# Attention scores on Trainium2: fp32 score products of two heads at once, or of one head each into the two halves of the PSUM rows

## The chip, the cores and the metric

The kernel runs on one core of one Trainium2 chip. The metric is the device time in microseconds, the median of several runs. A core has five engines that run side by side and meet at semaphores: TensorE (PE in the profile, with its weight loads in a row of their own, PEld), VectorE (DVE), ScalarE (ACT), GpSimd (POOL) and SyncE (SP), which here only issues DMAs.

## The reference

A gated cross-attention block with 32 sequences of 64 tokens, model width 512, followed by a gated expert layer. Cut to what matters here:

```python
q = (layernorm(x) @ wq)   # 32 heads of 128
k = (ctx @ wk)            # 8 heads of 128, each shared by 4 query heads
v = (ctx @ wv)
q, k = rope(q), rope(k)
raw = einsum('bhqd,bhkd->bhqk', q, k) / sqrt(128)     # 64 x 64 for each sequence and head
attn = softmax(raw + mask, axis=-1)
x = x + tanh(g_xattn) * (einsum('bhqk,bhkd->bhqd', attn, v) @ wo)
x = x + tanh(g_ffn) * experts(layernorm(x))           # top-1 of 8, rank 16
```

All of it is fp32. Most products are split by hand into a high and a low part (three products of type fp32r for each fp32 one); the score products are not: they take q and k as plain fp32.

## The kernel before, in words

A first stage (up to about 205 us of the profile) makes keys and values for all sequences, stores them to DRAM, and normalises and turns x. Then comes a loop of 64 steps (`STEPS`). A step k stands for one KV head (a group of four query heads), and four sequences (`SUB_SEQS`); two steps share the same eight sequences (`chunk`), and four steps the same half of the batch and the same KV head. 16 groups by 4 steps are the 64.

Each engine has its own program, written out by hand, and all waits are on named semaphores. On TensorE (from line 801) a step is, in this order: `scores(k)` (line 881), `times_values(k-1)` (line 909: probabilities of the step before by the values), one or two products of the next group's q projection (`product`, line 849), `project_out(k-1, 0)` (line 935: the first 128 tokens of the step before by wo), more of the q projection, `turn_probs(k)` (line 898: four transposes), `project_out(k-1, 1)`, and the last products of the projection (lines 1046 to 1072). The last four steps have an order of their own (lines 1074 to 1131), without projections. The expert layer's routing products (line 983) and its other pieces are put between these parts in some steps.

`scores(k)` waits for q and k of its group (semaphores `rope_added`, `k_in`) and until VectorE has taken the scores before (`masked`). The bank `score` has 128 partitions by 512 columns: partitions 0 to 63 hold the first head of a pair, partitions 64 to 127 the second, and the columns are two head pairs (`hp`) by four sequences (`b`) by 64 keys. For each of the 8 (hp, b), one call multiplies the queries of two heads (stationary, 128 rows of the head width by 2 x 64 columns) by the 64 keys of the sequence (moving). The last call increments `scored`.

VectorE waits for `scored` in `mask_scores` (line 1231; line 1241 scales and adds the mask, line 1246 finds the maximum), GpSimd subtracts it (line 1870), ScalarE takes the exponential (line 1613), VectorE sums and inverts (lines 1250, 1252), GpSimd multiplies (line 1875), and TensorE transposes the probabilities in `turn_probs`. The rope of q ends in line 1180 on VectorE.

`TWIN_ROWS` (line 44) is `(slice(0, SEQ), slice(SEQ, 2 * SEQ))`, the two halves of the partitions.

Of the kernel before, what the change touches and what calls it, by code (L numbers as in the profile page):

```python
# [14 lines left out]
BATCH, SEQ, DM = 32, 64, 512  # L15
# [28 lines left out]
TWIN_ROWS = (slice(0, SEQ), slice(SEQ, 2 * SEQ))  # L44
# [116 lines left out]
def products_of(k):  # L161

    G, r = divmod(k, 4)
    if G + 1 == GROUPS:
        return [[], [], []]
    b = HEAD_PAIRS * (G + 1) + r // 2
    lots = ((0, 1), (2,), (3,)) if r % 2 == 0 else ((4, 5), (), (6,) if k + 1 < WIDE else ())
    return [[(b, i) for i in lot] for lot in lots]
# [32 lines left out]
Q_SLOT, Q_BEFORE = {}, {}  # L201
# [91 lines left out]
def build(nc, x, ctx, mask, g_attn, g_ffn, wq, wk, wv, wo, routed_w, lora_b, table, out):  # L293
# [8 lines left out]
    with ExitStack() as stack:  # L302
        def bank(name):
            return stack.enter_context(nc.psum_tensor(name, [P, 512], F32))
# [4 lines left out]
        def sb_at(offset, name, shape, dt=F32):  # L309
            return nc.alloc_sbuf_tensor_at(name, shape, dt, offset=offset)  # L310
# [13 lines left out]
        k_r = sb_at(base + 28672, "k_r", [P, 2, CHUNK])  # L324
# [9 lines left out]
        q_r = [sb_at(base + place, f"q_r{i}", [P, CHUNK_SEQS, 2, SEQ])  # L334
               for i, place in enumerate((98304, 102400, 106496, 110592, 94208, 118784))]
# [52 lines left out]
        small, score, turned = bank("small"), bank("score"), bank("turned")  # L388
# [151 lines left out]
        def chunk_of(u):  # L540
            G, c = divmod(u, CHUNKS)
            return G, c, (G // KV_HEADS) * CHUNKS + c
# [258 lines left out]
        def _(e):  # L801
            drained = {}

            def free(b):

                if b.name in drained:
                    e.wait_ge(*drained[b.name])
# [73 lines left out]
            def scores(k):  # L881
                u, s = divmod(k, SUBS)
                G, c, index = chunk_of(u)
                e.wait_ge(rope_added, ROPE_NO["q", HEAD_PAIRS * G + 1, 1 if c == 0 else 3] + 1)
                e.wait_ge(k_in[u % 2], 16 * (u // 2 + 1))
                if k:
                    e.wait_ge(masked, k)
                free(score)
                for hp in range(HEAD_PAIRS):
                    for b in range(SUB_SEQS):  # L890
                        seq = s * SUB_SEQS + b
                        col = (hp * SUB_SEQS + b) * SEQ
                        two_heads = q_r[Q_SLOT[G, hp, c]][:, seq, :, :].rearrange("p h s -> p (h s)")
                        last = e.matmul(score[:, col:col + SEQ], two_heads, k_r[:, u % 2, seq * SEQ:(seq + 1) * SEQ],  # L894
                                        start=True, stop=True)
                last.then_inc(scored, 1)

            def turn_probs(k):
# [126 lines left out]
            for n in range(len(JOBS)):  # L1025
                make(n)
                if n == X_TURN:
                    e.wait_ge(table_in, 16)
                if n - X_TURN in X_BESIDE:
                    turn_x(X_BESIDE[n - X_TURN])  # L1030
                for b, i in Q_AFTER.get(n, ()):
                    product(b, i)
                if n == SCORES_AFTER:
                    drained[score.name] = rope_added, ROPE_NO[JOBS[-4]] + 1
                    scores(0)
# [3 lines left out]
            first, middle, last = products_of(0)  # L1039
            for b, i in first + middle:  # L1040
                product(b, i)
            turn_probs(0)
            scores(1)
            for b, i in last:
                product(b, i)
            for k in range(1, WIDE):
                first, middle, last = products_of(k)
                if k > 1:
                    scores(k)
                between(k, 0)  # L1050
                times_values(k - 1)
                between(k, 1)
                for b, i in first[:1]:
                    product(b, i)
                between(k, 2)
                for b, i in first[1:]:
                    product(b, i)
                between(k, 3)
                project_out(k - 1, 0)
                between(k, 4)  # L1060
                for b, i in middle:
                    product(b, i)
                turn_probs(k)
                between(k, 5)
                project_out(k - 1, 1)
                between(k, 6)
                for b, i in last[:1]:
                    product(b, i)
                between(k, 7)
                for b, i in last[1:]:  # L1070
                    product(b, i)
                between(k, 8)
# [959 lines left out]
```

## Time and profile before

| | us |
|---|---|
| median of 3 runs | 1091.02 |
| lowest, highest | 1090.81, 1091.05 |
| span of the profiled execution, first to last instruction | 1089.0 |
| busy in it: PE, PEld | 1082.4, 919.3 |
| busy: DVE, ACT, POOL | 874.1, 636.8, 591.9 |

The profile has one execution. The time of that execution outside its span isn't known by itself; the median of the runs is 2.0 us above the span. PE's busy time is that of matmuls as recorded: they are pipelined, one starts before the record of the one before has ended, and their ends are modelled, so the distance between starts tells more than a record's length. PEld (weight loads) goes on beside PE. A plain fp32 matmul call leaves two records on each of the two rows; a call of type fp32r leaves one. A chain of waits is followed back from the last instruction, at each step to what released it.

### The profile page before, as it was taken

How to read it: one execution, taken by the hardware profiler on the slowest of the kernel's cores; microseconds unless marked ns; L12 is line 12 of the kernel's file. 1: busy time of each engine (PE TensorE's matmuls, PEld its weight loads, DVE VectorE, ACT ScalarE, POOL GpSimd, SP SyncE). 2: the span in 40 equal slices, each digit the busy share in tenths (PEclk: the TensorE clock that was granted, in tenths of full speed). 3: DMA queues.
4: the chain of work that ended last, by engine and by line, in shares of the span. 5: the costliest groups of instructions: out<-in, count | busy, mean ns of one | idle time of the engine just before them, and what ended most of it. 6: DMA issues, size and time to landing. Idle time of an engine off the chain costs nothing.

```text
span 1089.0 us, 17107 instructions
## 1 busy us (share of the span) xinstructions
PE 1082.4 (99%) x5640; PEld 919.3 (84%) x5640; DVE 874.1 (80%) x1423; ACT 636.8 (58%) x1112; POOL 591.9 (54%) x518
## 2 busy tenths in 40 slices
PE   9999999999999999999999999999999999999998
PEld 7888888888888888888888888888888888888886
DVE  7876657888888888888887898777777777777887
ACT  7563476586666666666655545555555555555553
POOL 5552379888877777777754433333333333333423
PEclk9999999999999999999999999999999999999999
DMA  7858964496646464646489546553535353543112
GB/s 258 273 210 336 391 220 183 155 379 201 214 155 213 155 213 156 212 156 212 141 300 380 185 136 205 177 187 111 187 110 187 112 184 114 179 116 118 40 39 78
DMA packets 106087, 206.27 MB, mean 189 GB/s; under 512 B 8849, under 2 KB 58641, under 8 KB 100113
## 3 DMA queue, kind: packets, MB, share of 16 engines
q1 hardware_dynamic: 105424, 204.40, 55.2%
q8 instruction: 47, 0.77, 0.3%
q10 hardware_dynamic: 576, 0.79, 0.2%
q14 instruction: 40, 0.32, 0.1%
HBM read 122.31 MB, written 82.84 MB: 188 GB/s over the span
## 4 chain that ended last, share of the span: by engine, by line
PE 97%; DVE 2%; DMA 0%; issue 0%; ACT 0%; DVEq 0%; SPq 0%
PE attn L945 32%; PE proj L877 28%; PE score L894 10%; PE attn L839 8%; PE score L839 4%; PE turned L839 4%; PE attn L930 3%; PE attn L932 3%; PE turned L905 3%; PE proj L811 1%; PE small L983 1%; PE small L1008 1%; PE score L983 0%; DMA near_raw<-in_ctx 0%; DVE o_s L1270 0%; DVE stats L1140 0%
## 5 line engine op out<-in xcount | busy, mean ns | idle before, releaser
L945 PE MATMUL attn<-wo_s,o_s 128*128 128x512 f32 x1524 | 374.7, 395 | 0.2 <-DVE o_s L1270 0.2
L877 PE MATMUL proj<-xB,wq_s 128*128 128x512 f32 x1344 | 332.6, 391 | 0.0
L945 PEld LDWEIGHTS attn<-wo_s,o_s 128*128 128x128 f32 x1524 | 280.9, 188 | 57.0 <-DVE o_s L1270 0.4
L877 PEld LDWEIGHTS proj<-xB,wq_s 128*128 128x128 f32 x1344 | 252.0, 188 | 51.3 <-issue 0.2
L1863 POOL TENSOR_TENSOR rot<-rot,tab 128x512 f32<-128x512 f32 x110 | 162.3, 1475 | 145.2 <-ACT rot L1584 145.0
L1633 ACT ACTIVATE o_s<-attn 128x512 fp32r<-128x512 f32 x127 | 69.3, 595 | 112.2 <-PE attn L932 112.1
L894 PEld LDWEIGHTS score<-k_r,q_r 128*128 128x128 f32 x1024 | 123.9, 191 | 5.5 <-DVE q_r L1180 0.4
L1175 DVE TENSOR_TENSOR q_r<-q_r,tab 128x512 f32<-128x512 f32 x127 | 120.9, 952 | 1.5 <-ACT x_third L1584 1.4
L894 PE MATMUL score<-k_r,q_r 128*128 128x64 f32 x1024 | 121.3, 271 | 0.0
L1605 ACT ACTIVATE copies<-proj 128x512 f32<-128x512 f32 x96 | 57.5, 599 | 78.0 <-PE proj L877 77.8
L1282 DVE SCALAR_TENSOR_TENSOR acc<-attn,gates_t,acc 128x512 f32<-128x512 f32 x127 | 94.8, 747 | 4.1 <-PE attn L945 1.2
L1863 POOL TENSOR_TENSOR rot_third<-rot_third,tab 128x512 f32<-128x512 f32 x40 | 61.3, 1533 | 57.6 <-ACT rot_third L1584 54.8
L1262 DVE TENSOR_TENSOR p_low<-turned,p_high 64x512 fp32r<-64x512 f32 x128 | 87.7, 686 | 5.2 <-ACT p_high L1621 2.8
L1621 ACT ACTIVATE p_high<-turned 64x512 fp32r<-64x512 f32 x128 | 75.6, 590 | 23.5 <-PE turned L905 21.8
L1583 ACT ACTIVATE rot<-q_r 64x512 f32<-64x512 f32 x84 | 52.4, 623 | 52.5 <-DVE q_r L1219 51.4
L1270 DVE TENSOR_TENSOR o_s<-attn,o_s 128x512 fp32r<-128x512 f32 x127 | 81.4, 680 | 1.8 <-ACT o_s L1633 1.7
L1624 ACT ACTIVATE p_high<-p_high 64x512 fp32r<-64x512 f32 x128 | 80.8, 631 | 2.8
L1219 DVE TENSOR_TENSOR q_r<-copies,proj 128x512 f32<-128x512 f32 x127 | 81.1, 678 | 0.3 <-issue 0.3
L1180 DVE TENSOR_TENSOR q_r<-q_r,rot 128x512 f32<-128x512 f32 x85 | 69.2, 814 | 6.0 <-POOL rot L1863 0.3
L1241 DVE SCALAR_TENSOR_TENSOR prob_odd<-score,mask_sb 128x512 f32<-128x512 f32 x32 | 22.1, 691 | 52.7 <-PE score L894 52.6
L1870 POOL TENSOR_TENSOR prob_odd<-prob_odd,neg_max 128x512 f32<-128x512 f32 x32 | 33.7, 1053 | 54.9 <-DVE neg_max L1246 54.0
L1870 POOL TENSOR_TENSOR prob_even<-prob_even,neg_max 128x512 f32<-128x512 f32 x32 | 33.5, 1047 | 48.5 <-DVE neg_max L1246 48.5
(269 smaller groups left out, 1681.5 us busy)
## 6 DMA issues: line engine op xcount, KB each, us to landing
wq_kept<-wq_s SPq DMA_DIRECT2D x16, 1792.0 KB, 6.3
wq_s<-wq_kept SPq DMA_DIRECT2D x16, 1792.0 KB, 8.2
v_kept<-vst SPq DMA_DIRECT2D x64, 256.0 KB, 4.3
v_s<-v_kept SPq DMA_DIRECT2D x128, 128.0 KB, 5.0
wo_kept<-wo_s SPq DMA_DIRECT2D x32, 512.0 KB, 5.7
wo_s<-wo_kept SPq DMA_DIRECT2D x32, 512.0 KB, 5.2
k_kept<-kst SPq DMA_DIRECT2D x32, 256.0 KB, 2.2
wq_raw<-in_wq SPq DMA_DIRECT2D x16, 512.0 KB, 7.8
```

What stands on the lines that cost most here:

```text
L839: last = e.matmul(b[:, :], stationary, moving, start=(kt == 0 and m == 0), stop=(kt == KT - 1 and m == 2))
L877: last = e.matmul(dst[:, :], wq_s[:, b % 2, A, s, kt, :], xB[:, B, mv, kt, :], start=(first and kt == 0 and m == 0), stop=(kt == 1 and m = ...
L894: last = e.matmul(score[:, col:col + SEQ], two_heads, k_r[:, u % 2, seq * SEQ:(seq + 1) * SEQ], start=True, stop=True)
L945: last = e.matmul(out_bank(k, bp)[:, :], o_s[:, s, bp, h, :], wo_s[n % WO_SLOTS][:, m, :], start=(h == 0 and i == 0), stop=(h == GROUP - 1 ...
L1175: e.tensor_tensor(dst, src, cos, ALU.mult).then_inc(times_cos, 1)
L1219: e.tensor_tensor(q_tile(b, j) if dst is None else dst, by_seq(copies[:, copy, :]), by_seq(proj[PRODUCTS[i][2]][:, :]), ALU.add).then_inc( ...
L1262: e.tensor_tensor(p_low[rows, :, twin, :], turned[rows, :].rearrange("p (b n) -> p b n", b=PAIRS), p_high[rows, twin, :].bitcast(F32).rear ...
L1270: e.tensor_tensor(low, src, high.bitcast(F32), ALU.subtract).then_inc(out_low, 1)
L1282: e.scalar_tensor_tensor(out=acc[:, tile, :], in0=out_bank(k, bp)[:, :], scalar=gates_t[:, 0:1], in1=acc[:, tile, :], op0=ALU.mult, op1=AL ...
L1621: e.activation(p_high[rows, twin, :], turned[rows, :], ACT.Copy).then_inc(probs_high, 1)
L1624: last = e.activation(p_high[TWIN_ROWS[1 - twin], twin, :], p_high[rows, twin, :].bitcast(F32), ACT.Copy)
L1863: e.tensor_tensor(r3, r3, sin, ALU.mult).then_inc(times_sin, 1)
```

## The change

In `scores`, the call for two heads becomes two calls for one head each. The stationary operand has 64 columns instead of 128, the moving operand (the keys) is the same, and the output is the first or the second half of the bank's partitions. The semaphore increment stays on the last call.

```diff
@@ -890,9 +890,10 @@
                     for b in range(SUB_SEQS):
                         seq = s * SUB_SEQS + b
                         col = (hp * SUB_SEQS + b) * SEQ
-                        two_heads = q_r[Q_SLOT[G, hp, c]][:, seq, :, :].rearrange("p h s -> p (h s)")
-                        last = e.matmul(score[:, col:col + SEQ], two_heads, k_r[:, u % 2, seq * SEQ:(seq + 1) * SEQ],
-                                        start=True, stop=True)
+                        keys = k_r[:, u % 2, seq * SEQ:(seq + 1) * SEQ]
+                        for head, rows in enumerate(TWIN_ROWS):
+                            last = e.matmul(score[rows, col:col + SEQ], q_r[Q_SLOT[G, hp, c]][:, seq, head, :], keys,
+                                            start=True, stop=True)
                 last.then_inc(scored, 1)
```

## Rows read from the trace of the kernel before

**Rows 1.** The page: busy time with share and instructions, and slices of the span.

```profile
span 1089.0 us, 17107 instructions
PE 1082.4 (99%) x5640; PEld 919.3 (84%) x5640; DVE 874.1 (80%) x1423; ACT 636.8 (58%) x1112; POOL 591.9 (54%) x518
...
PE   9999999999999999999999999999999999999998
...
PEclk9999999999999999999999999999999999999999
```

**Rows 2.** The page: the chain that ended last, by engine and by line.

```profile
PE 97%; DVE 2%; DMA 0%; issue 0%; ACT 0%; DVEq 0%; SPq 0%
PE attn L945 32%; PE proj L877 28%; PE score L894 10%; PE attn L839 8%; PE score L839 4%; PE turned L839 4%; PE attn L930 3%; PE attn L932 3%; PE turned L905 3%; PE proj L811 1%; PE small L983 1%; PE small L1008 1%; PE score L983 0%; DMA near_raw<-in_ctx 0%; DVE o_s L1270 0%; DVE stats L1140 0%
```

**Rows 3.** Groups by shape on PE and PEld: count | busy us, mean ns | idle before.

```profile
L945 PE MATMUL attn<-wo_s,o_s 128*128 128x512 f32 x1524 | 374.7, 395 | 0.2 <-DVE o_s L1270 0.2
L877 PE MATMUL proj<-xB,wq_s 128*128 128x512 f32 x1344 | 332.6, 391 | 0.0
L894 PE MATMUL score<-k_r,q_r 128*128 128x64 f32 x1024 | 121.3, 271 | 0.0
...
L894 PEld LDWEIGHTS score<-k_r,q_r 128*128 128x128 f32 x1024 | 123.9, 191 | 5.5 <-DVE q_r L1180 0.4 <-issue 0.3
...
L905 PEld LDWEIGHTS turned<-tab,prob_even 128*128 128x128 f32 x128 | 15.7, 139 | 4.4 <-POOL prob_even L1875 0.4
```

**Rows 4.** The chain in order of time, 505 to 530 us: start, us, what.

```profile
506.35 0.44 PE turned L905 x4
506.79 2.77 PE attn L945 x12
509.56 1.36 PE proj L877 x6
510.92 1.73 PE score L894 x16
512.65 0.29 PE attn L930 x2
...
523.66 1.73 PE score L894 x16
```

**Rows 5.** Timeline of PE and PEld around one step's scores: start, us.

```profile
506.54 3.02 PE L945 MATMUL attn<-wo_s,o_s 128*128 128x512 f32 x12
509.40 1.52 PE L877 MATMUL proj<-xB,wq_s 128*128 128x512 f32 x6
510.76 1.89 PE L894 MATMUL score<-k_r,q_r 128*128 128x64 f32 x16
512.46 0.49 PE L930 MATMUL attn<-p_high,v_s 128*128 128x256 f32 x2
...
506.51 2.62 PEld L945 LDWEIGHTS attn<-wo_s,o_s 128*128 128x128 f32 x12
...
510.53 1.98 PEld L894 LDWEIGHTS score<-k_r,q_r 128*128 128x128 f32 x16
...
518.72 0.58 PEld L905 LDWEIGHTS turned<-tab,prob_odd 128*128 128x128 f32 x4
...
510.53 0.41 PEld L894 LDWEIGHTS score<-k_r,q_r 128*128 128x128 f32 x2
```

**Rows 6.** Routing products, fp32 with 136 columns: timeline, and their group by shape.

```profile
1079.68 1.09 PE L983 MATMUL score<-routedT,last_s 128*128 128x136 f32 x8
...
L983 PE MATMUL score<-routedT,last_s 128*128 128x136 f32 x8 | 1.1, 279 | 0.0
```

**Rows 7.** Timeline, the first products after TensorE's rest at 6 us.

```profile
6.46 0.30 PEld L839 LDWEIGHTS score<-ctxT,wk_s 128*128 128x128 f32 x2 [1.43 <-DVE ctxT L1170]
...
6.49 1.17 PE L839 MATMUL score<-ctxT,wk_s 128*128 128x512 f32 x4 [1.02 <-DVE ctxT L1170]
```

**Rows 8.** Waits (us in total, times, longest), and timeline of DVE and POOL at one step.

```profile
DVE prob_odd L1241 <- PE score L894: 52.6, 25, 2.3
...
DVE prob_even L1241 <- PE score L894: 24.3, 25, 1.6
...
508.75 0.67 DVE L1180 TENSOR_TENSOR q_r<-q_r,rot_third 128x512 f32<-128x512 f32 x1
...
512.69 0.69 DVE L1241 SCALAR_TENSOR_TENSOR prob_odd<-score,mask_sb 128x512 f32<-128x512 f32 x1 [1.76 <-PE score L894]
...
516.93 1.05 POOL L1875 TENSOR_TENSOR prob_odd<-prob_odd,row_inv 128x512 f32<-128x512 f32 x1 [0.46 <-DVE row_inv L1252]
```

**Rows 9.** Windows by stage: length, busy PE, PEld, DVE, ACT, POOL, clock, DMA share, GB/s.

```profile
205.00:1040.00 835.00, 834.74 (x4465) 714.10 (x4464) 685.83 (x1080) 498.62 (x864) 458.77 (x384) 1.00 0.54 180
```

## The prediction, made before the changed kernel ran

> **What bounds the kernel now.** I began with the page's busy table and its slices [rows 1]: TensorE is busy for 1082.4 of 1089.0 us at the full granted clock in all 40 slices, VectorE for 80%. The chain that ended last [rows 2] runs over TensorE for 97% and over the score products (line 894) for 10%. Busy TensorE is not TensorE at its peak, so the next view is the costliest groups by shape [rows 3]: the two big groups wait 0.2 us in all, so what the score products give or take on TensorE moves the end by the same amount, as long as nobody else becomes late. The chain in order of time [rows 4] shows one step of the loop: it comes back every 12.74 us (510.92 to 523.66), and 1.73 us of it are the score products. They are 8 calls and stand as 16 records, since each fp32 product is recorded as two weight loads and two matmuls. 64 steps by 1.73 us are 110.7 us, the chain's 10%.
>
> **What bounds the score products themselves.** The timeline of the two PE rows [rows 5] has 16 loads in 1.98 us. The second starts 0.23 us after the first (the two together end at 510.94, less one's 0.19 us), the last at 512.51 - 0.19 = 512.32, so 14 gaps cover 1.56 us: 0.111 us from load to load. What would the matmul alone need? The routing products are fp32 as well, with 136 columns [rows 6]: 8 records in 1.09 us, (1.09 - 0.28) / 7 = 0.116 us each, 0.85 ns per column; 64 columns would need 0.055 us. Their loads, of the same 128x128 as the score's, fit into those 0.116 us. So here the weight load sets the pace and the matmul half of the array's time is empty: per record 0.111 us of load against 0.055 us of stream. Instruction issue is not seen to bind: after rest a load starts at 6.46 and its matmul at 6.49, 0.03 us apart [rows 7]. That is just the pace that the change could ask for at best, so it stays a weak point.
>
> **The change, part by part.** Each of 512 products becomes two with 64 stationary columns instead of 128 and the same 64 moving columns. Records go from 16 to 32 a step on each PE row, 1024 to 2048 in all. The keys stream twice. The same rows and columns of the score bank are written in the end, the one semaphore increment still comes with the last product, and no wait, DMA or instruction of another engine is added or moved.
>
> Loads: no row shows a 64-column load. Bounds: 0.111 us each if a load costs the same whatever its width, 0.055 us if it goes by columns. I take 0.055, since two loads of the trace that differ only in mode (a transpose's, 139 ns, and a product's, 191 ns) [rows 3] show that the duration follows the amount that is moved and not a fixed price. Matmuls: 0.055 us each, as above.
>
> Without any overlap between the halves a step is 32 x 0.056 = 1.79 us against 1.73: +0.06 us. With overlap, where the product for rows 0 to 63 and that for rows 64 to 127 use different columns of the array at the same time, two records share a slot. The order is upper, upper, lower, lower (two records per call), so in order starts still allow it: the second record of one half runs beside the first of the other. That is 32 x 0.028 = 0.90 us. No row shows two products side by side, so the bounds are 0.90 and 1.79; I take 0.90 because there is nothing in common that is full: load and stream of one half fill their slot, and those of the other half are on other columns. The Trainium skill's page "TensorE: Matmul & The Clock Gate", section "Part 3: Packing small matmuls", measured 2.38x for three column tiles; scaled to two that is about 1.6x, 1.13 us a step by an estimate, which would halve my gain. No run here shows it.
>
> Switching: 64 times the array goes from whole to half use and back. Nothing in the trace switches. Lower bound 0, if the next load is taken in beside the running matmul, as the first score load is now (it starts at 510.53, and the matmul before it runs on to 510.76). Upper bound: the array is emptied. A matmul record of 512 columns lasts 0.39 us while the next one starts 2.77 / 12 = 0.23 us after it [rows 3, 4], so 0.16 us are its tail, and after rest the first weights lie open: four matmuls took 1.17 us where 3 x 0.23 + 0.39 = 1.08 are usual [rows 7], 0.09 us. Together 0.25 us per switch, 0.50 us per step. The Trainium skill's page "TensorEngine Tiling (Array Packing)", section "Key Properties", says that a change of tiling mode drains TensorE; that speaks for the upper end, and the trace can't confirm it. I take 0.15 us a switch, 0.30 a step, since the tail and the load may partly lie over each other.
>
> Sum per step: 0.90 + 0.30 = 1.20 us against 1.73, so 0.53 us less; by 64 steps 34 us.
>
> **Does it arrive?** VectorE takes the scores. It stood waiting for them in 25 + 25 steps for 52.6 + 24.3 us [rows 8], 1.5 us each, and in the step shown for 1.76 us. Scores that come 0.53 us sooner are taken sooner. From there mask, maximum, exponential and normalisation run until 516.93 + 1.05 = 517.98 [rows 8], and the transposes of the probabilities begin on TensorE with the load at 518.72 [rows 5]; both the chain and TensorE's other work begin at the end of the scores, so this slack of 0.7 us stays as it is. VectorE is busy 685.8 of 835 us between 205 and 1040 us [rows 9]; with 34 us less it stands at 86%. The rope sums that the next scores need end at 508.75 + 0.67 = 509.42 [rows 8], 1.1 us ahead of the first score load. If the cover goes, in the 14 steps where VectorE doesn't wait, about 3 us of the 34 are lost. Forecast: 31 us less. The sum is made against the profiled execution (span 1089.0 us); the median of the runs is 1091.0, 2 us around the span that stay. 1091 - 31 = 1060 us.
>
> **Rivals.**
> *The halves take turns and the switches are paid.* Place: lines 894 ff., 64 times. Step 1.79 + 0.30 = 2.09 us, +0.36 a step, +23 us, 1114 us; with the dear switch +0.56, +36 us, 1127 us; with a free one +4 us, 1095 us. It decides as soon as the overlap saves less than 1.79 + 0.30 - 1.73 = 0.36 us of its possible 0.89 us a step. For it: both halves take their keys and weights from all 128 rows, and the trace has no two records at work at once. Against: the halves share no column and no output row. Chance 0.27.
> *Load and matmul of one half no longer overlap, or a half load costs a whole one.* 0.055 + 0.055 = 0.111 us a record either way, 32 x 0.111 = 3.55 us, +1.82 us a step, +117 us, 1208 us. Against it: in the output projection 12 loads with 2.62 us of work lie within 3.02 us of matmuls on the same 128 rows [rows 5]. For it: that is the whole array, never a part. Chance 0.12. The same page's Part 3 has a rule of this kind, that a load overlaps a matmul in flight only where the row groups differ; taken at its word it gives these 1208 us, and the trace disagrees for the whole array.
> *It comes out even.* Partly overlapping halves eat exactly the switches: 1091 us. Chance 0.05.
> *Everything overlaps and switching is free.* 1.73 - 0.90 = 0.83 us a step, 53 us, 1038 us: the good end of the forecast's own case.
>
> **Numbers.** Forecast's case (overlap, switches partly paid) 0.56, turns 0.27, no overlap of load and matmul 0.12, even 0.05. The range leaves out the 0.12 and a few per cent of dear switches: 1038 to 1120 us. The likeliest case alone spans 1038 (free switches) to 1075 (0.25 us a switch, 0.33 us a step, and 5 us lost at VectorE). About 0.2%, 2 us, is what a measurement of this kernel can tell from no change. Faster 0.56, same 0.05, slower 0.39.
>
> **What would show it.** Right: in the chain the score products fall from 1.73 to about 1.2 us a step and the step from 12.74 to 12.2; matmul records of line 895 start under 0.04 us apart on the average; gaps of 0.1 to 0.2 us stand before the first score load's matmul and before the first matmul of line 930; VectorE's waits for the scores shrink by about 30 us. Overlap wrong: records 0.055 us apart through the whole stretch. Load step wrong: 0.11 us apart. If the score stretch shrinks and the step does not, look for a new wait before the transposes of the probabilities or before the scores. The granted clock should stay at 2.4 GHz.

## The result and the profile after

| | before | changed |
|---|---|---|
| median, us | 1090.91 | 1064.24 |
| lowest to highest | 1090.63 to 1091.05 | 1063.76 to 1064.26 |
| span of the profiled execution | 1089.0 | 1062.4 |
| busy PE, PEld | 1082.4, 919.3 | 1052.3, 864.8 |
| busy DVE, ACT, POOL | 874.1, 636.8, 591.9 | 872.4, 637.6, 591.9 |

The ratio is 0.9751, with a 95% interval of 0.9737 to 0.9765: faster by 2.5%, 26.7 us. The forecast was 1060 us, with a range of 1038 to 1120. Line numbers from 895 on are one higher than before.

The chain that ended last, on the page of the changed kernel, first by engine, then by line:

```profile
PE 85%; DVE 6%; POOL 4%; issue 2%; ACT 1%; DMA 1%; SPq 1%; DVEq 0%; ACTq 0%; POOLq 0%
PE attn L946 30%; PE proj L877 25%; PE attn L839 7%; PE score L895 6%; PE score L839 4%; PE turned L839 4%; PE attn L931 3%; PE turned L906 2%; PE attn L933 2%; POOL wq_s L1839 1%; PE proj L811 1%; POOL rot L1864 1%; DVE acc L1283 1%; DVE q_r L1176 1%; DVE o_s L1271 1%
```

The score products went from 10% of the chain to 6% [rows 2]. The new thing is in the first line: TensorE holds 85% of it where it held 97%. In some stretches the chain now runs over other engines, and that is where a part of the gain turns out to be lost.

The two groups of the score products (out of the groups by shape; `128*64` are the active rows and columns of the array):

```profile
L895 PEld LDWEIGHTS score<-k_r,q_r 128*64 128x64 f32 x2048 | 64.9, 138 | 22.7 <-issue 20.5 <-DVE q_r L1181 2.2
L895 PE MATMUL score<-k_r,q_r 128*64 128x64 f32 x2048 | 73.7, 225 | 0.4 <-DVE prob_even L1242 0.4
```

Twice as many records, half the columns, and PE is busy with them for 73.7 us instead of 121.3 [rows 3]. A load's record shrank from 191 to 138 ns. The 20.5 us of idle "issue" ahead of the loads are new.

The chain in order of time, the step that answers to [rows 4]:

```profile
501.78 1.36 PE proj L877 x6
503.14 1.08 PE score L895 x32
504.23 0.43 PE attn L931 x2
504.66 0.23 PE attn L933
...
515.40 1.08 PE score L895 x32
```

The score products take 1.08 us instead of 1.73, the first two products by the values 0.43 instead of 0.29; together 0.51 us less. The step is 515.40 - 503.14 = 12.26 us instead of 12.74.

The timeline of PE and PEld over the same place, where [rows 5] show the old one, then close looks at its start (all of one kernel and view, with ever narrower windows):

```profile
502.53 0.61 PE L877 MATMUL proj<-xB,wq_s 128*128 128x512 f32 x2
503.07 0.28 PE L895 MATMUL score<-k_r,q_r 128*64 128x64 f32 x2
...
503.07 1.15 PE L895 MATMUL score<-k_r,q_r 128*64 128x64 f32 x32
504.15 0.50 PE L931 MATMUL attn<-p_high,v_s 128*128 128x256 f32 x2
...
502.75 0.39 PE L877 MATMUL proj<-xB,wq_s 128*128 128x512 f32 x1
503.07 0.27 PE L895 MATMUL score<-k_r,q_r 128*64 128x64 f32 x1
...
503.07 1.01 PEld L895 LDWEIGHTS score<-k_r,q_r 128*64 128x64 f32 x32 [0.35 <-issue]
504.15 0.30 PEld L931 LDWEIGHTS attn<-p_high,v_s 128*128 128x128 f32 x2
...
503.07 0.14 PEld L895 LDWEIGHTS score<-k_r,q_r 128*64 128x64 f32 x2 [0.35 <-issue]
```

Read the starts. 32 matmuls start between 503.07 and 503.07 + 1.15 - 0.22 = 504.00 us, 0.03 us apart on the average. They come in pairs: the first alone lasts 0.27 us and the first two together 0.28, so the second starts 0.01 us after the first. The second pair starts at 503.18, 0.11 us after the first, and from there a pair starts every 0.058 us (504.00 - 503.18 = 0.82 over 14 distances). That distance is called a slot from here on: 32 records in pairs are 16 slots. At both ends the weights are no longer fetched ahead. Before, the first score load started at 510.53, together with the last matmul of the projection, 0.23 us ahead of its own matmul; now load and matmul start together at 503.07, 0.32 us after that matmul (502.75). The same on the way out: load and matmul of line 931 start together at 504.15, 0.15 us after the last score matmul, where a slot is 0.058.

VectorE's waits for the scores (us in total, times, longest):

```profile
DVE prob_odd L1242 <- PE score L895: 34.7, 25, 1.7
...
DVE prob_even L1242 <- PE score L895: 12.7, 13, 1.1
```

They fell from 76.9 to 47.4 us [rows 8].

### The profile page after: what moved, and what is told of

It reads as the page before. It is cut to its first block, busy times and chain, and to the rows that moved or that the text cites. A ratio compares the mean times of both kernels' runs of the same rounds, so it can differ in the third digit from the quotient of the medians.

```text
span 1062.4 us, 19155 instructions
## 1 busy us (share of the span) xinstructions
PE 1052.3 (99%) x6664; PEld 864.8 (81%) x6664; DVE 872.4 (82%) x1423; ACT 637.6 (60%) x1112; POOL 591.9 (56%) x518
## 4 chain that ended last, share of the span: by engine, by line
PE 85%; DVE 6%; POOL 4%; issue 2%; ACT 1%; DMA 1%; SPq 1%; DVEq 0%; ACTq 0%; POOLq 0%
PE attn L946 30%; PE proj L877 25%; PE attn L839 7%; PE score L895 6%; PE score L839 4%; PE turned L839 4%; PE attn L931 3%; PE turned L906 2%; PE attn L933 2%; POOL wq_s L1839 1%; PE proj L811 1%; POOL rot L1864 1%; DVE acc L1283 1%; DVE q_r L1176 1%; DVE o_s L1271 1%
## 5 line engine op out<-in xcount | busy, mean ns | idle before, releaser
L1622 ACT ACTIVATE p_high<-turned 64x512 fp32r<-64x512 f32 x128 | 75.6, 590 | 25.9 <-PE turned L906 24.2
L895 PEld LDWEIGHTS score<-k_r,q_r 128*64 128x64 f32 x2048 | 64.9, 138 | 22.7 <-issue 20.5
L895 PE MATMUL score<-k_r,q_r 128*64 128x64 f32 x2048 | 73.7, 225 | 0.4 <-DVE prob_even L1242 0.4
L931 PE MATMUL attn<-p_high,v_s 128*128 128x256 f32 x254 | 57.7, 309 | 1.6 <-DVE p_low L1263 0.8
L1876 POOL TENSOR_TENSOR prob_even<-prob_even,row_inv 128x512 f32<-128x512 f32 x32 | 34.1, 1066 | 44.0 <-DVE row_inv L1253 44.0
L1876 POOL TENSOR_TENSOR prob_odd<-prob_odd,row_inv 128x512 f32<-128x512 f32 x32 | 35.8, 1118 | 38.4 <-DVE row_inv L1253 38.4
```

The costliest lines, as they stand in the source:

```text
L895: last = e.matmul(score[rows, col:col + SEQ], q_r[Q_SLOT[G, hp, c]][:, seq, head, :], keys, start=True, stop=True)
L931: e.matmul(b[:, cols[twin]], v_s[:, u % 2, twin, tiles[bp], :], p_high[:, twin, cols[bp]], start=(twin == 0), stop=False, skip_group_check ...
```

## The experiments

All are edits of the changed kernel unless it is said otherwise. The times stand beside runs of the kernel before on the same chip.

**Do the halves work side by side, and how far ahead are they found?** Three kernels change the order of the 16 half products of a step alone.

Run e1, all upper ones first:

```diff
-                for hp in range(HEAD_PAIRS):
-                    for b in range(SUB_SEQS):
...
-                        for head, rows in enumerate(TWIN_ROWS):
+                for head, rows in enumerate(TWIN_ROWS):
+                    for hp in range(HEAD_PAIRS):
+                        for b in range(SUB_SEQS):
```

> The 16 half products of a step in another order: the 8 for rows 0 to 63 first, then the 8 for rows 64 to 127; nothing else differs from the changed kernel. Theory A (two halves work side by side, only neighbours find each other): 32 records at 0.058 us instead of 16 pairs at 0.058, the stretch from first to last start grows from 0.93 to about 1.81 us, +0.88 us by 64 steps = +56 us, about 1120 us, slower than the kernel before. Theory B (a half product is simply cheap, 0.029 us a record wherever it stands): 1064 us. Theory C (side by side, with a queue for each half that reaches over 16 records): 1064 us too, and then the starts still come in pairs.

Run e2, runs of two calls for each half:

```diff
-                    for b in range(SUB_SEQS):
...
-                        for head, rows in enumerate(TWIN_ROWS):
+                    for two in range(0, SUB_SEQS, 2):
+                        for head, rows in enumerate(TWIN_ROWS):
+                            for b in (two, two + 1):
```

> Order upper, upper, lower, lower, so runs of four records for one half. Theory A with starts strictly in order: only the last record of a run has a partner, 32 - 7 = 25 slots of 0.058 us, the stretch 1.4 us, +0.47 us a step, about 1094 us. Theory A with a reach of at least four records: pairs as in the changed kernel, stretch 0.93 us, 1064 us. Theory B: 1064 us. The trace tells the two apart: pairs 6 ns apart, or even distances.

Run e12 came later, with the reach that these two had shown: runs of four calls.

```diff
-                    for b in range(SUB_SEQS):
...
-                        for head, rows in enumerate(TWIN_ROWS):
+                    for head, rows in enumerate(TWIN_ROWS):
+                        for b in range(SUB_SEQS):
```

> Halves in runs of four calls (eight records): four upper, four lower, four upper, four lower. The reach of the pairing: four records found their partner (e2), and with 16 in a run only the last three did (e1). If the reach is about three to four records, each of the three borders in a step hides about three or four slots: 32 - 10 = 22 slots, stretch 1.25 us, +0.32 us a step, about 1085 us. If it is eight or more: 1064 us.

| run | median, us | ratio to before, 95% |
|---|---|---|
| e1 upper then lower | 1106.78 | 1.0144 (1.0127 to 1.0160) |
| e2 two and two | 1067.25 | 0.9782 (0.9767 to 0.9797) |
| e12 four and four | 1085.13 | 0.9943 (0.9930 to 0.9957) |

The score pieces of their chains in order of time, from about 500 to 510 us. Of e1:

```profile
502.56 1.83 PE score L895 x32
504.39 0.44 PE attn L931 x2
```

Of e2:

```profile
503.76 1.13 PE score L896 x32
504.89 0.44 PE attn L932 x2
```

Of e12:

```profile
509.27 1.47 PE score L895 x32
510.74 0.43 PE attn L931 x2
```

The same 2048 loads and matmuls of the same shapes, only in another order, cost 1.08, 1.13, 1.47 or 1.83 us a step. So a half product is not simply cheap (theory B is out), and no queue reaches over 16 records (theory C is out too): with the halves far apart, the edit is slower than the kernel before, by 1.4%. What counts is a partner in the other half near enough. The strict order of starts, on which my sum rested, is out as well: with two and two it would have cost 25 slots, and it costs 1.13 us against 1.08. The reach is limited: e12 takes 0.39 us more than the changed kernel, at 0.058 us a slot seven slots more, 23 in all, so each of its three borders hid three records (32 - 9); and e1, with one border, takes 0.75 us more, 13 slots, again three hidden (32 - 3 = 29 against 16). In e2 the runs of four records found nearly all their partners: 17 slots, one more than the changed kernel. That e1 came out at 1107 and not at the 1120 of theory A: 0.75 x 64 = 48 us over 1064 would be 1112, but e1 doesn't lose again what the changed kernel has already lost to other engines in its first and last steps (below). Its scores of step 7 start at 297.88, only 1.7 us behind the changed kernel's 296.14 (seven steps by 0.75 would be 5.3); from there to step 60 it falls behind by 39.5 us, 0.745 a step.

**What does a switch between whole and half products cost?** Runs e3 and e4 have the same work, half of it as half products, half of it as whole ones, with two or with eight switches a step. The diff is e3's; in e4 the condition is `b % 2 == 0`.

```diff
+                        if hp == 0:
                             for head, rows in enumerate(TWIN_ROWS):
...
+                        else:
+                            two_heads = q_r[Q_SLOT[G, hp, c]][:, seq, :, :].rearrange("p h s -> p (h s)")
+                            last = e.matmul(score[:, col:col + SEQ], two_heads, keys, start=True, stop=True)
```

> First head pair as half products (8 calls), second head pair as four products of both heads: two switches a step as in the changed kernel. Halves: 8 pairs at 0.058 = 0.46 us; whole ones: 8 records at 0.111 = 0.89 us. With switches of about 0.08 us each, 0.1 to 0.2 us a step less than before, 6 to 12 us less, 1079 to 1085 us. It is the base for the next run.

> The same 8 half and 4 whole products as in the run before, but alternating by sequence: eight switches a step instead of two. Price of a switch as read from the changed kernel's trace, 0.08 us: 6 x 0.08 x 64 = +31 us over the run before, about 1112 us. Price as forecast, 0.15 us: +58 us, about 1140 us. The array emptied in full, 0.25 us: +96 us. Switching free: no difference.

e3 took 1087.32 us (0.9967, 0.9954 to 0.9980), e4 1141.59 us (1.0462, 1.0447 to 1.0478). Chain in order of time of e3:

```profile
510.18 0.61 PE score L896 x16
510.79 1.03 PE score L900 x8
```

and of e4, where the first four of eight pieces stand:

```profile
501.09 0.27 PE score L896 x4
501.36 0.36 PE score L900 x2
501.72 0.27 PE score L896 x4
501.99 0.36 PE score L900 x2
```

In these a step's scores take 0.61 + 1.03 = 1.64 us in e3 and 4 x (0.27 + 0.36) = 2.52 us in e4. Six more switches cost 0.88 us, 0.147 us each. The time says the same: 54.3 us by 64 by 6 is 0.141 us. The 0.08 us of the expectations had been read from the gaps at both ends of the stretch and were too little: a switch also costs inside the stretch. The starts of e4 show both parts. At a change the next matmul starts 0.205 us (whole to half) or 0.151 us (half to whole) after the last one, where 0.111 and 0.058 are usual, so 0.09 us more; and the second record behind it, or the second pair, comes another 0.05 us late (0.160 for 0.111, 0.100 for 0.052). Together that is 0.14 us. e3 missed its expectation for the most part for that reason: 1.73 - 1.64 = 0.09 us a step are 5.8 us, or 1085; the other 2 us were not followed up.

**What sets the slot of 0.058 us, load or stream?** e5 cuts the load to 32 columns (four quarters of the PSUM rows), e8 cuts the stream to 32 columns.

```diff
-                        for head, rows in enumerate(TWIN_ROWS):
-                            last = e.matmul(score[rows, col:col + SEQ], q_r[Q_SLOT[G, hp, c]][:, seq, head, :], keys,
-                                            start=True, stop=True)
+                        for quarter in range(4):
+                            rows, part = slice(32 * quarter, 32 * quarter + 32), slice(quarter % 2 * 32, quarter % 2 * 32 + 32)
+                            last = e.matmul(score[rows, col:col + SEQ], q_r[Q_SLOT[G, hp, c]][:, seq, quarter // 2, part],
+                                            keys, start=True, stop=True)
```

> Each product of two heads as four calls of 32 stationary columns, written to the four quarters of the PSUM rows: 64 records a step on each row of TensorE. If the stream of 64 columns sets a slot (0.058 us) and four quarters work side by side, a product still takes 2 x 0.058 us and nothing changes: 1064 us. If the load sets the slot, it halves with the columns: the stretch falls from 0.93 to about 0.5 us, 0.4 x 64 = 27 us less, 1037 us. If four at once are not kept busy by issue, or only two go side by side: the stretch up to 1.86 us, 1124 us.

```diff
-                            last = e.matmul(score[rows, col:col + SEQ], ..., keys,
+                            last = e.matmul(score[rows, col:col + SEQ // 2], ..., keys[:, 0:SEQ // 2],
```

> The changed kernel with 32 moving columns instead of 64 in the score products; the scores of the second half of the keys are left out. Loads as in the changed kernel (64 columns). If the load sets the slot of 0.058 us: no difference, 1064 us. If the stream sets it: the slot falls to about 0.03 us, the stretch from 0.93 to about 0.5 us, 27 us less, 1037 us. If load and stream are equally long, as the columns say: no difference here and none with the quarters.

e5: 1062.28 us (0.9736, 0.9723 to 0.9750). e8: 1063.16 us (0.9743, 0.9728 to 0.9757). Timeline of PE in e5:

```profile
514.15 1.10 PE L896 MATMUL score<-k_r,q_r 128*32 128x64 f32 x64
```

and in e8:

```profile
515.17 1.12 PE L895 MATMUL score<-k_r,q_r 128*64 128x32 f32 x32
```

The loads of the same two stretches, e5's first:

```profile
514.15 0.94 PEld L896 LDWEIGHTS score<-k_r,q_r 128*32 128x32 f32 x64 [0.35 <-issue]
```

```profile
515.17 1.01 PEld L895 LDWEIGHTS score<-k_r,q_r 128*64 128x64 f32 x32 [0.35 <-issue]
```

The changed kernel has 1.15 us of matmuls and 1.01 us of loads. With half the stream the loads still take 1.01 us: their starts keep the slot of 0.058 us, and the 0.03 us that the matmuls gain lie in the first pair alone (0.08 us to the second instead of 0.11). So it isn't the stream that sets the slot. With half the load the slot falls only to 0.056 us, which is about what a stream of 64 columns needs by the routing products (0.055). That fits a load that sets the slot in the changed kernel, with a stream 0.002 to 0.003 us shorter right behind it. It is not shown, however, that columns are the reason for both: a fixed price of just under 0.06 us for each record of a part would look nearly the same in e5 and e8, and no run halves load and stream together. Four quarters do go side by side: 64 records in 1.10 us.

e9 and e10 put the changed kernel and the quarters side by side again, and e11 adds a first try at the paced steps (next part) with nothing left out:

```diff
-        return w[1] <= GROUP or w[1] % GROUP == 3
+        return w[1] <= GROUP + 2 or w[1] % GROUP == 3
```

> The changed kernel itself, on the same chip as the next two, to measure small differences against: 1064.2 us.

> The quarters again beside the changed kernel: their slot is 0.055 instead of 0.058 us, the stretch 0.88 instead of 0.93 us, 0.05 x 64 = 3.1 us, of which the paced first steps give none: 1061 to 1062.5 us, 2 us under the run before. If the difference of the earlier runs was one of chips or of transfers: none.

> The quarters, and the low parts of the wo rows of heads 5 and 6 on VectorE instead of GpSimd (steps 3 and 4), so that nothing is left out. If GpSimd's backlog alone paces steps 2 to 7, up to 2.5 us less than the run before, 1060 us. If VectorE, busy for nine tenths there, is as near to being late, it gives the gain back: no difference, or up to 1 us slower.

| run | median, us | lowest to highest | ratio to before, 95% |
|---|---|---|---|
| e9 changed kernel | 1063.80 | 1063.61 to 1064.27 | 0.9749 (0.9736 to 0.9762) |
| e10 quarters | 1062.27 | 1061.62 to 1068.70 | 0.9746 (0.9724 to 0.9767) |
| e11 quarters, relief | 1063.02 | 1062.19 to 1063.54 | 0.9743 (0.9729 to 0.9756) |

The quarters' medians lie 1.5 to 2 us under the changed kernel's both times, but one of their runs took 1068.7 us and the intervals overlap: it can't be called a gain in time, though the trace has each step of the middle 0.05 us shorter. Moving the two wo rows to VectorE gave nothing; in the stretch from step 2 to step 7 it took 0.4 us more than e10 (67.82 against 67.42), with VectorE busy for 85.3 of the 95 us between 205 and 300 instead of 81.9.

**Where is the rest of the gain?** The sum of a step, 0.51 us less, would be 32.6 us in 64 steps; 26.6 arrived in the span. The starts of the scores in steps 7 and 60 tell where it went. PE's timeline at these places, of the kernel before:

```profile
295.88 1.33 PE L894 MATMUL score<-k_r,q_r 128*128 128x64 f32 x11
...
1024.42 0.78 PE L894 MATMUL score<-k_r,q_r 128*128 128x64 f32 x6
```

and of the changed one:

```profile
296.14 1.03 PE L895 MATMUL score<-k_r,q_r 128*64 128x64 f32 x28
...
998.77 1.15 PE L895 MATMUL score<-k_r,q_r 128*64 128x64 f32 x32
```

After seven passes of scores the changed kernel is 0.26 us behind, not 3.6 us ahead: 3.9 us are gone. From step 7 to step 60 it gains 25.9 us, 0.49 a step. The four passes from step 60 on would be 2.0 us; from a lead of 25.65 to one of 26.6 it is 0.95. In sum 32.6 - 3.9 - 53 x 0.02 - 1.1 = 26.5 us.

The starts of the scores, read in the same way for more steps (us):

| start of the scores of step | 0 | 2 | 7 | 60 | 62 |
|---|---|---|---|---|---|
| before | 204.58 | 228.04 | 295.88 | 1024.42 | 1035.32 |
| changed | 204.94 | 228.68 | 296.14 | 998.77 | 1009.51 |
| e9, the changed kernel again | 204.59 | 228.07 | 295.54 | 998.23 | 1008.97 |
| e6, less work for GpSimd (below) | 204.65 | 228.17 | 293.68 | 996.37 | 1007.10 |

Of the 3.9 us, 0.36 are there before the first scores start (204.94 against 204.58), and they are no effect of the change: e9, the same kernel, starts them at 204.59. TensorE's wait for its first operands, in the changed kernel's list of waits,

```profile
PEld score L839 <- DVE ctxT L1171: 1.9, 1, 1.9
```

was 1.43 us before [rows 7]. Another 1.3 us go in steps 0 and 1, 0.75 of them in one wait for VectorE that the kernel before doesn't have:

```profile
217.18 0.36 PE L931 MATMUL attn<-p_high,v_s 128*128 128x256 f32 x1 [0.75 <-DVE p_low L1263]
```

The remaining 2.2 us go in steps 2 to 6, which take 67.46 us instead of 67.84, where 2.55 less was to be had. For these see the longest pieces of the changed kernel's chain between 205 and 300 us:

```profile
204.84 4.55 DMA raw<-in_wo
223.51 2.94 POOL wq_s L1839 x2
233.80 3.02 PE attn L946 x12
238.62 2.79 PE attn L946 x12
254.74 3.77 POOL wq_s L1839 x3
```

Before, the chain of that stretch was TensorE's alone. Runs e6 and e7 shorten just that work in the changed kernel and in the kernel before; the low parts of half the columns of wq blocks 3 to 7 are left out:

```diff
                 e.wait_ge(wq_high, 4 * b + piece + 1)
+                if HEAD_PAIRS < b < HEAD_PAIRS + 6:
+                    low, src, high = (ap[..., 0:DH // 2] for ap in (low, src, high))
                 e.tensor_tensor(low, src, high.bitcast(F32), ALU.subtract).then_inc(wq_low, 1)
```

> The changed kernel, with the low parts of the wq blocks 3 to 7 on GpSimd (line 1839, steps 0 to 9) made for half of their columns; the rest is left out. In the changed kernel's trace steps 2 to 7 keep the old pace. If GpSimd's backlog is what holds them, the 0.5 us a step comes back there: about 3 us less, 1061 us. If VectorE or the transfers of that stretch hold them: 1064 us, no difference.

> The same edit in the kernel before, as a control. There TensorE waits for nobody in these steps, so both theories say no difference: 1091 us. If this one falls too, the relief acts on something else.

e6: 1061.66 us (0.9733, 0.9720 to 0.9746), 2.1 to 2.6 us less than the changed kernel. The intervals of the ratios overlap, but e6's four runs took 1061.5 to 1062.8 us and the changed kernel's eight (e9 with them) 1063.6 to 1064.3. e7: 1090.96 us (1.0002, 0.9993 to 1.0010), nothing. In e6 step 7's scores start at

```profile
293.68 1.15 PE L895 MATMUL score<-k_r,q_r 128*64 128x64 f32 x32
```

2.46 us sooner than in the changed kernel. 0.29 of that was there at the first scores and 0.22 came in steps 0 and 1; steps 2 to 6 take 65.51 us instead of 67.46, so 1.95 of the 2.2 us lost there come back. The same relief is worth nothing while TensorE is the slowest and about 2 us once it is not: a cover that was just long enough before. The wait of step 1 stays in e6 (0.72 us); no run tried it.

The last steps show where 0.8 of the 1.1 us went. From the scores of step 60 to those of step 62 the kernel before takes 10.90 us and the changed one 10.74, where two steps should gain 1.0. TensorE has two waits there that the kernel before has not:

```profile
1001.42 0.28 PE L895 MATMUL score<-k_r,q_r 128*64 128x64 f32 x2 [0.36 <-DVE prob_even L1242]
...
1006.16 0.33 PE L906 MATMUL turned<-tab,prob_even 128*128 128x128 f32 x1 [0.59 <-POOL prob_even L1876]
```

Here the scores of step 61 come right behind the products by the values, without projections between, so VectorE has less time to take the scores of step 60; and the transposes of step 60 wait until GpSimd has normalised its probabilities. No run tests this.

## Why the prediction was right

**What bounds the scores: right.** Loads of 128 columns at 0.111 us each, with the stream half as long, was the reading. With loads of 64 columns and the same stream the distance halves, and in e8 half the stream leaves it at 0.058 us. e5 has the next bound at 0.056 us, so after the change load and stream are nearly balanced.

**A half load costs half: right.** 138 ns a record instead of 191, and in e1 13 more slots cost 0.75 us, 0.058 us each (0.055 forecast). The reason given for it was weak: the two loads of 139 and 191 ns have the same 128x128 shape, so they say nothing about columns. The choice of the lower bound came true without having been shown.

**The halves overlap: right, its order wrong.** "In order starts still allow it: the second record of one half runs beside the first of the other" was the argument; the trace shows pairs from the first record on, and e2 that the partner may stand four records later. The size was unharmed, 16 slots or 17. The estimate of 1.13 us a step that stood beside the sum was too dear: the 32 starts lie within 0.93 us. The rival in which the halves take turns is what e1 is, by hand.

**The switches: right.** 0.15 us taken, 0.147 and 0.141 measured. The value was picked between bounds of 0 and 0.25 us, so that it came this close is partly luck; its bounds were a tail of 0.16 us and first weights of 0.09, and the starts show 0.09 us before the first record and 0.05 before the second. That these two are the tail and the weights isn't shown. The 0.09 us are seen on the way in (0.32 against 0.23 from the last projection matmul to the first score one) and on the way out (0.15 against 0.058). The Trainium skill's page "TensorEngine Tiling (Array Packing)", section "Key Properties", has TensorE drain at a change of mode. The trace agrees in so far as no load is taken ahead over a change any more, and the loads' 20.5 us of idle "issue" are new; whether the array is emptied it can't tell, since the first half load starts at 503.07 and the record of the matmul before it, whose end is modelled, runs to 503.14.

**The step: right.** 0.53 us less was forecast for the scores with their switches; 0.51 came in the chain of the step shown. VectorE's waits shrank by 29.5 us, "about 30" was said, and the clock stayed at full speed.

**What is lost at other engines: too small.** This is the term that was mis-sized: 3 us for steps in which VectorE doesn't wait, against 6 us. The 3 us had no working behind them (14 such steps by 0.53 us would be 7.4). They are 3 of the 4.3 us by which the forecast of 31 us less was missed; the other 1.3 are the scores, 0.02 us a step. I looked for cover in VectorE's waits over the whole loop and in one step of the middle. The first eight steps, where GpSimd still works off its splits, have another balance: in the kernel before, GpSimd is busy for 77.87 of 95 us between 205 and 300, and for 364.42 of 700 after that. 3.9 us stayed there: 0.4 are a later start, 1.3 went in steps 0 and 1, and of the 2.2 in steps 2 to 6 e6 gives 2.0 back. About 1 us went in the last four steps, whose order is another. There the slack of 0.7 us before the transposes, which the prediction held to stay as it is, is gone: TensorE waits 0.59 us for GpSimd's probabilities. The trace shows these waits; no run has taken them away. That the measured time lies well inside the range says little, since the range of 1038 to 1120 us also held the rival in which the halves take turns.

**Loads beside matmuls of the same rows: the rival fell.** The Trainium skill's page "TensorE: Matmul & The Clock Gate", "Part 3: Packing small matmuls", has a bullet that allows it only for different row groups, and that would have given 1208 us; the same section's "The mechanism" also lets a load go ahead into a background weight buffer. Here 32 loads lie in 1.01 us beside 1.15 us of matmuls, all of them on 128 rows. The measurement decides against the bullet; by which way the loads get in, no run shows.

## What to carry to other kernels

Where a matmul's moving side takes less time than its weight load, look at the distance of the loads: if it is more than the stream needs, cut the stationary side into halves with PSUM rows of their own, and issue the halves alternately, since a partner more than a few records away is not found and the edit then loses. Each change between whole and half products costs 0.15 us, so keep the half ones together: two switches for eight products paid, eight switches did not. And when the slowest engine gets faster, look for the stretch of the loop where another one has least to spare; the mean over the loop, or one step of its middle, hides it.

## What was not expected

The two halves are fed from a look-ahead, not strictly in program order: two start 0.01 us apart from the first record on, even where four records for the same half stand first, as in this timeline of e2:

```profile
516.00 0.28 PE L896 MATMUL score<-k_r,q_r 128*64 128x64 f32 x2
```

The records don't name their half; that the two are one of each is inferred from e1, where records of the same half start 0.058 us apart. And the look-ahead ends after three or four records (e1, e12). Four quarters of 32 columns run at once without loss, with 64 loads and 64 matmuls started in about 0.9 us, 7 ns apart on the average; issue, the weak point of the argument, is far from a bound here.
